# The order of VectorE's work in a windowed-attention batch: the last inversion and the maxima are moved

## The reference, cut to what matters

```python
xn = _layernorm(x, axis=-1)                      # x: 8 batches x 512 tokens x 256
x = x + attn(xn, w_qkv, b_qkv, w_out, b_out) + ffn(xn, w12, w3, gate_w)

# attn: 16 heads of 16, windows of 128 keys, each 64 tokens further on
scores = jnp.einsum('bhnqd,bhnkd->bhnqk', qw, kw) / jnp.sqrt(jnp.float32(D))
probs = jax.nn.softmax(scores, axis=-1)
ow = jnp.einsum('bhnqk,bhnkd->bhnqd', probs, vw)
o = ow.transpose(0, 2, 3, 1, 4).reshape(b, nw * W, c)
o = o @ w_out + b_out
return o[:, :l, :]                               # only the first 512 rows are kept

# ffn: the top 2 of 8 experts for each token, silu(h1) * h2, weighted by a softmax of the two gates
```

## Time and profile before

| what | value |
|---|---|
| median of 3 runs | 704.7 us (702.45 to 705.29) |
| the profiled execution, its own time | 704.97 us |
| its span, first to last instruction | 703.2 us |
| TensorE matmuls busy | 630.0 us, 90% |
| TensorE weight loads busy | 509.7 us, 72% |
| VectorE busy | 567.5 us, 81% |
| ScalarE busy | 513.2 us, 73% |
| GpSimd busy | 281.5 us, 40% |
| mean granted TensorE clock | 0.981 of full speed |

### The profile page before, as it was taken

One profiled execution on the slowest core, in us unless ns is written; L12 is line 12 of the kernel. 1 busy time (PEld: TensorE's weight loads), 2 busy tenths in 40 slices (PEclk: granted clock), 3 DMA queues, 4 the chain that ended last, 5 costly groups with the idle time before them and its releaser, 6 DMA issues.

```text
span 703.2 us, 17940 instructions
## 1 busy us (share of the span) xinstructions
PE 630.0 (90%) x5914; PEld 509.7 (72%) x5915; DVE 567.5 (81%) x902; ACT 513.2 (73%) x882; POOL 281.5 (40%) x330
## 2 busy tenths in 40 slices
PE   0786785989999999999999999999999999999985
PEld 0554564765888888888888888888767676666663
DVE  4968899986888888888888888888587979788884
ACT  4554578396787787777877877777577788888885
POOL 3000274033344444444544544444201336666654
PEclk9998789899999999999999999999999999999999
DMA  9795478491111111111111111111178778885740
GB/s 299 263 257 193 110 251 305 121 314 48 53 52 52 60 52 52 59 48 57 53 52 60 52 53 60 52 52 54 38 192 242 180 246 209 262 228 159 207 141 31
DMA packets 66337, 92.62 MB, mean 132 GB/s; under 512 B 6432, under 2 KB 53408, under 8 KB 66272
## 3 DMA queue, kind: packets, MB, share of 16 engines
q1 hardware_dynamic: 57904, 70.56, 33.8%
q0 software_dynamic: 6816, 18.62, 7.9%
q10 hardware_dynamic: 1568, 2.76, 1.2%
HBM read 58.93 MB, written 32.83 MB: 130 GB/s over the span
## 4 chain that ended last, share of the span: by engine, by line
PE 65%; DVE 14%; ACT 10%; issue 7%; POOL 2%; DMA 1%; ACTq 0%; DVEq 0%; POOLq 0%
PE PS L1319 57%; PE PS L1570 4%; DVE SMALL L980 4%; ACT WORK L785 3%; PE PS L1548 2%; DVE XN L1138 2%; DVE WALL L974 2%; ACT QS L780 1%; DMA XN<-in_x 1%; DVE WORK L1049 1%; DVE WORK L1042 1%; ACT WORK L723 1%; DVE WALL L998 1%; ACT SIDE L792 1%; POOL OTS L595 1%
## 5 line engine op out<-in xcount | busy, mean ns | idle before, releaser
L367 DVE TENSOR_TENSOR WS<-WALL,WS 128x1024 fp32r<-128x1024 f32 x134 | 164.4, 1227 | 55.2 <-ACT WS L877 40.8
L1319 PE MATMUL PS<-WS,XTS 128*128 128x512 f32 x804 | 203.9, 402 | 0.0
L1319 PEld LDWEIGHTS PS<-WS,XTS 128*128 128x128 f32 x804 | 146.2, 189 | 30.5
L877 ACT ACTIVATE WS<-WALL 128x1024 fp32r x134 | 141.6, 1056 | 8.8 <-issue 0.3
L1319 PE MATMUL PS<-DOWN_HIGH,HTS 128*128 x568 | 115.9, 289 | 0.8 <-ACT HTS L892 0.8
L595 POOL TENSOR_TENSOR OTS<-SIDE,XN 128x256 f32<-128x256 f32 x30 | 22.8, 761 | 205.2 <-DVE XN L1138 138.5
L1319 PEld LDWEIGHTS PS<-DOWN_HIGH,HTS 128*128 128x128 f32 x568 | 90.9, 188 | 1.6 <-issue 1.5
L980 DVE TENSOR_REDUCE SMALL<-PS 128x8 f32<-128x1024 f32 x64 | 77.5, 1211 | 12.2 <-PE PS L1319 11.9
L785 ACT ACTIVATE WORK<-PS 128x512 f32<-128x512 f32 x128 | 69.4, 595 | 23.6 <-PE PS L1319 20.3
L667 POOL DMA_INDIRECT ys_scratch<-SIDE,SIDX x36 | 43.8, 1218 | 93.2 <-ACT SIDE L908 93.2
L663 POOL DMA_INDIRECT XS<-xn_scratch,GIDX x71 | 71.8, 1011 | 23.0 <-issue 21.3
(11 more groups left out here) (147 smaller groups left out, 1090.9 us busy)
## 6 DMA issues: line engine op xcount, KB each, us to landing
WALL<-in_wexp SPq DMA_DIRECT2D x28, 384.0 KB, 7.1
WALL<-ys_scratch SPq DMA_DIRECT2D x16, 512.0 KB, 7.2
parts_scratch<-WORK SPq DMA_DIRECT2D x32, 240.0 KB, 2.4
QS<-parts_scratch SPq DMA_DIRECT2D x16, 480.0 KB, 4.6
XN<-in_x SPq DMA_DIRECT2D x4, 1024.0 KB, 12.1
xn_scratch<-XN SPq DMA_DIRECT2D x4, 1024.0 KB, 7.3
WALL<-in_x SPq DMA_DIRECT2D x8, 512.0 KB, 5.9
KS<-parts_scratch SPq DMA_DIRECT2D x16, 240.0 KB, 4.1
```

What stands on the lines that cost most here:

```text
L367: eng.tensor_tensor(out=WS[:, 1 - k, half, 1], in0=weights, in1=WS[:, 1 - k, half, 0].bitcast(F32), op=ALU.subtract).then_inc(low_ready[ha ...
L877: act.activation(WS[:, 1 - k, half, 0], weights, ACT.Copy).then_inc(high_ready[half], 1)
L1319: return pe.matmul(o, a, b, start=start, stop=stop)
```

## The change

VectorE's program is reordered; no operation is added or taken away, and no other engine's program is touched.

- `split` is cut in two. Its first half (the subtraction to REST) stays ahead of the maximum. Its second half, `finish_split` (the cast and the second subtraction), now comes behind `take_max`, in units 0 to 3 of batches 0 to 6.
- `invert` for a batch's last query block moves from unit 0 of the next batch, behind that unit's maximum, to the end of unit 7, behind unit 7's `project`. This holds after batches 0 and 2 to 6. Batches 1 and 7 end in another way (`ends`) and keep theirs.

```diff
@@ -1045,6 +1045,11 @@
                     link(rest)
                 else:
                     rest.then_inc(w_free, 1)
+
+            def finish_split(n, first=False):
+
+                blk = BLOCKS[n]
+                if not first:
                     dve.wait_ge(w_free, c["W"].now() + 1)
                 link(dve.tensor_copy(PARTS[:, 1, blk, :], REST))
                 tt(PARTS[:, 2, blk, :], REST, PARTS[:, 1, blk, :], ALU.subtract).then_inc(parts_ready, 1)
@@ -1077,6 +1082,7 @@
             variance(2)
             for n in range(4):
                 split(n, True)
+                finish_split(n, True)
             normalise(2)
@@ -1203,7 +1209,9 @@
                         split(u)
                     if not (last and u >= UNITS - 3):
                         take_max()
-                    if u in (2, 4, 6) or (u == 0 and pending):
+                    if not last and u < 4:
+                        finish_split(u)
+                    if u in (2, 4, 6):
                         invert()
@@ -1238,6 +1246,8 @@
                         invert_halves()
                     if u % 2 == 1 and u > 1:
                         project(b, u // 2 - 1)
+                if not ends(b):
+                    invert()
                 if not last:
                     c["W"].add(NWIN)
```

## The result

The changed kernel takes 706.59 us in the median of 20 runs (702.87 to 710.28), the kernel before 704.52 us on the same chips (20 runs, 702.45 to 705.58). The ratio is 1.0032, 95% interval 1.002 to 1.0043: about 2 us slower, where the prediction had 1 us faster. It lies inside the predicted range. The runs also spread more, over 7.4 us instead of 3.1.

The account below looks back on a forecast made before the run. VectorE was taken to set the pace in units 0 to 3, with the stack chain through DRAM limiting the gain. Terms -2.4 + 0.7 + 0.6 = -1.1 us gave 703.6 us; likeliest case 701 to 708, wider range 699.5 to 707.8.

Parts of the forecast that it names:

- Step 1: Inversion for the last query block moved behind unit 7's projection sum: 1.66 us put into VectorE's idle time, batches 3 to 6.
- the old gap: VectorE's 2.11 us idle at the head of a batch, until ScalarE has made the first part.
- Step 2: Maximum ahead of the cast and second subtraction: score banks free 0.77 us earlier in 28 units, parts 1.54 us later.
- The port term: GpSimd's earlier adds slow VectorE's cast and subtraction in unit 0 through shared ports: 0.4 us taken, between 0 and 1.2.
- 0.90 us to spare: In batch 4, time between the last KS load's landing (596.66) and unit 6's score product that needs it (597.56).
- Batches 1 and 2: Later parts without step 1's gain: loss 0.6 us in batch 1 (0.3 to 1.5), 0.7 in batch 2 (0 to 1.5).
- C: Rival, chance 0.12: GpSimd's adds, started 4 us sooner, block VectorE in unit 0; 706.7 us, up to 710.4.
- A: Rival, chance 0.14: stacks do not hold unit 6's product back, so VectorE's shorter row gains 8.2 us; 696.5 us.
- B: Rival, chance 0.14: lateness eats exactly the 0.90 us spare; batches 3 to 6 give 0.3, 1 and 2 take it; 704.7.
- The range's upper end: All bounds on the slow side, 1.2 + 3.0 = +4.2 us, given as 708 in the likeliest case's range of 701 to 708.

Follow-up runs that it names:

- the inversion alone: The changed kernel with the maxima put back behind the parts in units 0 to 3, keeping only the moved inversion; 699.61 us, ratio 0.9933.
- the first profile: Profiled execution of the unaltered changed kernel from its first measurement, 703.72 us; a rerun of the same kernel gave the second, 705.0 us.
- the ladder of units: Kernels differing from the changed one only in which units take the maximum before finishing the part; from 698.01 us (unit 0) to 706.59 us (units 0 to 3).
- the maxima alone: The changed kernel with the inversion put back in unit 0, keeping only the maximum ahead of the part's finish; 707.75 us, ratio 1.0048.
- the copies first: The changed kernel with unit 2's copies issued ahead of the first half's loads on SP; 711.88 us, ratio 1.0112.

## Why the prediction was wrong, step by step

- **Step 1, right in mechanism.** The reciprocal lies in the old gap, 1.74 us for the 1.66 forecast; ScalarE's wait for OTS in unit 1 is gone; the division is 4.3 us earlier in its batch for 4 forecast. Taken alone it is worth 5 us, of the 6.6 that four batches of 1.66 would give.
- **Step 2's order, right; its price, mis-sized.** The weight loads' waits for the maximum fell from 24.3 to 5.3 us. But this wait was no cost: the inversion alone keeps 22.0 of it and gains most.
- **The port term** was taken as 0.4 us between 0 and 1.2. The cast and the subtraction of unit 0 lost 0.53 and 0.45, and the small cast 0.11 (0.28 for 0.17): 1.1 us, near its upper bound. But unit 1's cast and subtraction got 0.73 back at once. The last part was not 0.3 us later in its batch: in batches 3 to 6 it was ready at 18.0 to 18.1 us, for 18.1, 18.6, 18.7 and 18.7 before.
- **The steps that failed** are two. The first is **"The last part is then 0.3 us later than before, with 0.90 us to spare: the unit-6 product can start 0.6 us earlier"**, which carried 4 x 0.6 of the sum. It took the way from last part to landing as a constant, 7.6 us. In batches 3 to 6 of the first profile it is 8.5, 8.5, 8.8 and 7.8 us from the part's issue to the product that waits for it (621.88 to 630.67 in batch 5), and 8.6, 9.1, 7.7 and 8.4 in the second: 0.8 us more on the average, nearly the whole spare. The constant hid two parts: SP stands at L409 until unit 2's copies are down, and these stand behind the first half's loads, which go by unit 1's part. The prediction counted the delay of the last part and of no other; by the ladder of units, the delay of unit 1's part costs 4 us, and unit 3's 3. That the product still starts 2.2 and 2.0 us earlier in all, for 2.4 forecast, is luck: an earlier part made up for a longer way.
- The second is **"TensorE has four pieces of work without a gap there, so this stays"**, for the 6.74 us from that product to the next batch. In the two profiles it is 8.06, 8.03 and 7.95 us in three batches of eight, since the granted clock falls to half behind the wait. The sum had no term for it; 1.6 us in the first profile and 3.1 in the second.
- **Batches 1 and 2.** Loss 0.6 and 0.7 forecast. In the profiles batch 2 loses 0.23 and 0.13. Batch 1 waits 2.17 and 2.07 us; from its first projection to unit 6's product it takes 40.7 and 39.2 us for 38.7, a loss of 2.0, above its upper bound of 1.5, or of 0.5.
- **The rivals.** The sign was C's and the 706.7 it gives is the median, but its mechanism is ruled out by the kernel with the new order in unit 0 alone, where the adds block VectorE all the same (0.86 and 0.94 us in its batch 5) and the time is 698.0. A ("the stacks do not hold the product back", 696.5) is wrong for the changed kernel; the inversion alone comes nearest to it. B contradicts itself: it lets the spare be eaten exactly and still counts 0.3 us a batch.
- **The range's upper end** is off by its own sum: 704.7 + 4.2 is 708.9 and not 708. The measured time does not hang on it.
- **What the profile would show** came in part as written: TensorE's idle time in unit 6, released by a KS load, in batches 1 to 6. What did not follow is that the batch falls by 0.6: the starts of batches 2 and 6 are 132.97 us apart for 132.56.

Of the 2 us, then: step 1 alone gives 5 (shown); unit 1's and unit 3's later parts take 7 back (shown by the ladder). Of these, 4.3 come back when the wait for the second half's stack is taken away, together with the half-clock stretches behind it; 2.7 do not. How the 4.3 are shared between waiting and clock is open. That the delay runs from unit 1 through the loads and unit 2's copies rests on the landings and on the kernels that move the copies; no kernel shows it by a gain. Open too are where the median's loss lies, since the two profiles of the changed kernel took 703.72 and 705.0 us and that of before 704.97, and the wide spread of its times, which fits a landing and a clock that vary from execution to execution but was not followed run by run.

The best version measured finishes the parts of units 1, 2 and 3 ahead of the maximum and has both the moved inversion and the new order in unit 0: 698.01 us, 0.9921 of before. It is not told apart from the inversion alone (0.9933) by these intervals.

## What to carry to other kernels

A chain through DRAM (parts out, stacks back) is no constant behind its last link. Each link that the issuing engine waits for in order, and each transfer that its queue already holds, can set the landing; so when an order is changed, follow every block's part to its landing, not only the last one's. An engine's waits for a neighbour in the profile (24 us for the maximum here) are no price list: see first whether the stretch gets shorter when the wait's cause is left and another is taken away. A wait that is moved to where TensorE was busy can cost more than its length, if the clock falls behind it. Two moves in one edit are worth timing apart, since here one gave 5 us and the other took 7.

## What the runs showed of the hardware

- Copies of 80 to 240 KB from SBUF to DRAM, unit 2's: with no loads issued just ahead of them they landed in 1.8 to 3.7 us (batches 2 to 6 with the copies first), close behind 0.96 MB of loads in 3.5 to 5.5 us (the same batches after), and in 2.5 to 4.5 us before, where the loads are 0.3 to 0.9 us ahead. The last part's 240 KB landed in 2.1 to 2.8 us after, and in 4.5 to 5.1 right behind the loads.
- The granted clock of TensorE went to half behind single waits of 1.8 to 2.1 us, in stretches in which it was otherwise busy, and cost 1.5 to 1.6 us each time; behind a wait of 3.09 us the way on was 9.30 us for 6.5. Other waits of the same length did not do it: 1.83 us in batch 3 and 2.17 in batch 1 after, 2.04 in batch 4 with the maxima alone, 2.26 in batch 4 with the copies first.
- VectorE beside GpSimd's adds: a 128x320 cast 0.86 us for 0.33, a subtraction 0.94 for 0.49.
